# Mamba stage: the drive of every second pair of states made by VectorE in PSUM, with B spread by DMA, and A and the dt bias loaded plainly and placed by TensorE

## What is computed

```python
xz = h @ in_proj_w
u, z = jnp.split(xz, 2, axis=-1)
u = silu(causal_depthwise_conv(u, conv_w, conv_b))
xdbl = u @ x_proj_w                      # dt_r (64), B (16), C (16)
dt = softplus(dt_r @ dt_proj_w + dt_proj_b)
A = -jnp.exp(A_log)
def step(hst, inp):
    dt_t, B_t, C_t, u_t = inp
    dA = jnp.exp(dt_t[..., None] * A)
    dBu = dt_t[..., None] * B_t[:, None, :] * u_t[..., None]
    hst = dA * hst + dBu
    y = jnp.einsum('bdn,bn->bd', hst, C_t)
    return (hst, y)
y = (ys + u * D) * silu(z)
return y @ out_proj_w
```

## Time and profile before

| | |
|---|---|
| median of 3 runs | 2992.26 us (2989.83 to 2993.07) |
| the profiled execution | 2989.16 us, its span 2987.4 us |
| first scan starts | 814.89 us |
| scan of position 0 of the last item | 2618.08 us |
| mean clock granted to TensorE, of full speed | 0.961 |
| PE, DVE, ACT, POOL busy, share of the span | 89%, 79%, 62%, 61% |

### The profile page before, as it was taken

The page is one execution under the profiler, slowest core; times in us unless marked ns, Lnnn a source line. Parts: engine busy times, 40 slices in busy tenths (PEclk is TensorE's granted clock), DMA queues, the critical chain, the costliest instruction groups (busy, mean ns, idle before and its releaser), DMA issues. The chain is left out here.

```text
span 2987.4 us, 48154 instructions
## 1 busy us (share of the span) xinstructions
PE 2668.5 (89%) x17342; PEld 2127.1 (71%) x17342; DVE 2348.1 (79%) x2434; ACT 1848.3 (62%) x2524; POOL 1826.3 (61%) x1211
## 2 busy tenths in 40 slices
PE   5999996596699999999999999999999999985892
PEld 4878785464277878878778788777787887874561
DVE  6878874574389889899888898998988988894563
ACT  3565653254567777777677776776777767761451
POOL 1221211454477877878778787787787877784454
PEclk8999998798799999999999999999999999998896
DMA  1211212424402112022020120210202202103333
GB/s 49 64 49 56 63 36 56 112 75 116 159 1 78 47 39 86 9 79 73 14 86 23 64 86 1 85 64 23 86 8 79 86 1 78 45 27 89 90 103 102
DMA packets 137133, 186.07 MB, mean 62 GB/s; under 512 B 27800, under 2 KB 112664, under 8 KB 136920
## 3 DMA queue, kind: packets, MB, share of 16 engines
q1 hardware_dynamic: 129432, 162.69, 17.8%
q0 software_dynamic: 7488, 20.46, 2.7%
HBM read 141.13 MB, written 41.98 MB: 61 GB/s over the span
## 5 line engine op out<-in xcount | busy, mean ns | idle before, releaser
L1353 POOL TENSOR_TENSOR m_state<-m_state,m_c_all 128x1024 f32<-128x1024 f32 x512 | 1205.1, 2368 | 357.3 <-DVE m_state L1468 356.3
L1468 DVE TENSOR_TENSOR_SCAN m_state<-m_decay,m_ps_d 128x1024 f32<-128x1024 f32 x512 | 1162.1, 2278 | 145.0 <-issue 89.0
L1533 ACT ACTIVATE m_decay<-m_dt,m_aneg 128x511 f32<-128x511 f32 x1024 | 657.7, 710 | 30.1 <-DVE m_state L1468 26.6
L1768 PEld LDWEIGHTS m_ps_d<-m_bdiag,m_duT 128*128 128x128 f32 x4096 | 488.4, 192 | 105.9 <-issue 73.4
L1781 PE MATMUL m_ps_y<-m_ident,m_state 128*128 128x128 f32 x4096 | 533.1, 273 | 3.0 <-POOL m_state L1353 2.5
L1768 PE MATMUL m_ps_d<-m_bdiag,m_duT 128*128 128x128 f32 x4096 | 504.5, 276 | 29.4 <-DVE m_state L1468 23.6
L1781 PEld LDWEIGHTS m_ps_y<-m_ident,m_state 128*128 128x128 f32 x4096 | 463.6, 141 | 8.7 <-POOL m_state L1353 7.5
L1445 DVE TENSOR_TENSOR m_duB<-m_duT,m_ps_i 128x1024 f32<-128x1024 f32 x256 | 306.1, 1196 | 8.8 <-ACT m_duT L1561 8.8
L1766 PEld LDWEIGHTS m_ps_d<-m_ident,m_duB 128*128 128x128 f32 x2048 | 235.5, 141 | 76.9 <-issue 70.9
L1679 PE MATMUL m_ps_f<-m_hT,m_win 128*128 128x512 f32 x512 | 249.8, 612 | 36.0 <-ACT m_u L1574 17.9
L1766 PE MATMUL m_ps_d<-m_ident,m_duB 128*128 128x128 f32 x2048 | 265.8, 273 | 7.1 <-DVE m_state L1468 7.0
(11 more groups left out here) (201 smaller groups left out, 4407.0 us busy)
## 6 DMA issues: line engine op xcount, KB each, us to landing
m_c_all<-m_c_rows SPq DMA_DIRECT2D x128, 512.0 KB, 5.5
out<-m_xw SPq DMA_DIRECT2D x32, 512.0 KB, 2.9
f_y_rows<-f_y_sb SPq DMA_DIRECT2D x46, 256.0 KB
a_xin<-x SPq DMA_DIRECT2D x16, 512.0 KB, 4.8
a_xres<-x SPq DMA_DIRECT2D x16, 512.0 KB, 5.6
x<-a_xout SPq DMA_DIRECT2D x16, 512.0 KB, 3.3
m_xin<-x SPq DMA_DIRECT2D x16, 512.0 KB
m_xw<-out SPq DMA_DIRECT2D x16, 512.0 KB, 5.6
```

Of the source, the lines that this page charges most:

```text
L1353: nc.gpsimd.tensor_tensor(s, s, c_all[:, n, :, :], ALU.mult).then_inc(weighed, 1)
L1468: nc.vector.tensor_tensor_scan(state[:, r, :, :].rearrange("p n t -> p (n t)"), decay[:, r, :, :].rearrange("p n t -> p (n t)"), ps_d[i % ...
L1533: ins = nc.scalar.activation(decay[:, r, j, 1:S], dt_sb[:, c, 1:S], ACT.Exp, scale=aneg[:, c, n:n + 1])
L1768: ins = nc.tensor.matmul(drive_t, duT[:, c, t, :], bdiag[:, n // 2, TT * j + t, :], start=True, stop=True)
```

## The change

**Drives.** At even positions DVE now writes the drive itself: du, with channels on partitions, is copied by ScalarE into a PSUM bank (ps_u, `put_du`, once for each chunk), B of the pair stands in SBUF on all 128 partitions (b_all), and `scale` multiplies the two into ps_d[0]. TensorE makes only the odd positions, all into ps_d[1]. The 8 transposes at every even position are gone, and with them duB. dt and duT keep 2 chunks instead of 4.

**B.** It goes to DRAM beside C (8 small stores an item instead of 4) and comes back by 4 more DMAs of 512 KB an item (`b_pair`), each behind a `c_pair` in SP's queue.

**Diagonals.** DVE makes none. POOL makes two of the four tiles of an item at its positions 26 and 28, ScalarE the other two at its positions 0 and 3, each by 8 copies of 128x128 with B as scale.

**Start.** A_log and the bias are loaded as they lie, and TensorE places them by 20 small matmuls; 17 DMAs go, 2 come. Several parts of DVE, POOL and ScalarE stand one to three positions earlier or later.

```diff
@@ TURNS (also X, Y1, B, DT0 and O1 one later)
-        16: [("O", 0, -1)],
+        17: [("O", 0, -1)],
@@ start, SP
-            for r in range(Q):
-                for k in range(CT):
-                    sp.dma_start(aneg[CH * r:CH * r + CH, k, :].rearrange("c (q g) -> c q g", q=Q),
-                                 a_log[:, Q * k + r, :].rearrange("(c q) g -> c q g", q=Q)).then_inc(a_loaded, 16)
@@ SP
+            def b_pair(m):
+
+                sp.dma_start(b_all[:, m, :, :], bc_rows[0, 4 * m:4 * m + 2, :].partition_broadcast(P))\
+                    .then_inc(b_loaded[m], 16)
...
                     for n in range(NP - 2):
                         c_pair(st, 1, n)
+                        if n % 2 == 0:
+                            b_pair(n // 2)
@@ POOL
+                    if i in (26, 28) and st.has(1):
+                        diagonal(st, 1, i - 25)
@@ DVE
-                nc.vector.tensor_tensor(duB[:, r, :, :, :], duT[:, c, :, :].unsqueeze(1).to_broadcast([P, 2, TT, P]),
-                                        ps_bt[h][:, 2 * n:2 * n + 2, :].unsqueeze(3).to_broadcast([P, 2, TT, P]),
-                                        ALU.mult).then_inc(scaled, 1)
+                if n == 0:
+                    dve.wait_ge(du_put, CT * b + c + 1)
+                if c == 0:
+                    dve.wait_ge(b_loaded[n // 2], 16 * (b + 1))
+                if i >= 2 or st.has(o - 1):
+                    dve.wait_ge(scanned, UN * b + i - 1)
+                nc.vector.tensor_tensor(ps_d[0][:, :, :], ps_u[:, :].unsqueeze(1).to_broadcast([P, 2, S]),
+                                        b_all[:, n // 2, :, :], ALU.mult).then_inc(scaled, 1)
...
-                    if i % 2 and i + 3 < UN and st.has(0):
-                        scale(st, 0, i + 3)
-                    if i % 2 and i + 3 >= UN and st.has(1):
-                        scale(st, 1, i + 3 - UN)
+                    if i % 2 == 0 and i + 2 < UN and st.has(0):
+                        scale(st, 0, i + 2)
...
-                    if i in (23, 30) and st.has(1):
-                        dt_relu(st, 1, (23, 30).index(i))
-                    if i in (26, 28, 30) and st.has(1):
-                        diagonal(st, 1, i - 25)
+                    if i in (24, 30) and st.has(1):
+                        dt_relu(st, 1, (24, 30).index(i))
+                    if i == 30 and st.has(1):
+                        scale(st, 1, 0)
@@ ScalarE
+            def put_du(st, o, c):
+
+                b = st.item(o)
+                act.wait_ge(du_ready, CT * b + c + 1)
+                if c or st.has(o - 1):
+                    act.wait_ge(scaled, UN // 2 * b + NP // 2 * c)
+                nc.scalar.activation(ps_u[:, :], du_sb[:, c % 2, :], ACT.Copy).then_inc(du_put, 1)
...
+                for j in range(2):
+                    for t in range(TT):
+                        ins = nc.scalar.activation(bdiag[:, n // 2, TT * j + t, :], id_sb[:, :], ACT.Copy,
+                                                   scale=bt[h][:, 2 * n + j, t:t + 1])
...
+                    if i == 29 and st.has(1):
+                        put_du(st, 1, 0)
+                    if i in (0, 3) and st.has(0):
+                        diagonal(st, 0, 5 if i == 0 else 7)
@@ TensorE
-                    if i < UN - 1 and st.has(0):
+                    if i % 2 == 0 and st.has(0):
                         drive(st, 0, i + 1)
-                    if i == UN - 1 and st.has(1):
-                        drive(st, 1, 0)
```

More of the change, by code:

```diff
@@ L1464, in emit @@
                         dve.wait_ge(decay_ready, g + 1)
-                        dve.wait_ge(drive_full, g + 1)
+                        dve.wait_ge(drive_full if i % 2 else scaled, UN // 2 * st.item(0) + i // 2 + 1)
                         if i >= RING or st.has(-1):
@@ L1479, in emit @@
                         y_read(st, 0, (i - 9) // 8)
-                    if i == 0 and st.has(0):
-                        diagonal(st, 0, NP - 1)
                     if i in (9, 17) and st.has(0):
@@ L1485, in emit @@
                         gate(st, -1, 3)
-                    if i in (17, 23) and st.has(-1):
-                        b, v = st.item(-1), (i - 17) // 6
+                    if i in (18, 24) and st.has(-1):
+                        b, v = st.item(-1), (i - 18) // 6
                         dve.wait_ge(res_back, 16 * (b + 1))
@@ L1616, in emit @@
                         silu(st, z_sb, "Z", z_full, z_ready, (0, 1) if i == 25 else (2, 3))
-                    if i in (2, 12, 20) and st.has(0):
-                        to_duT(st, 0, 1 + (2, 12, 20).index(i))
-                    if i == 19 and st.has(1):
+                    if i in (2, 12, 21) and st.has(0):
+                        to_duT(st, 0, 1 + (2, 12, 21).index(i))
+                    if i == 20 and st.has(1):
                         b = st.item(1)
@@ L1626, in emit @@
                         nc.scalar.activation(xd[0:RX, :], f_bank("X", 0)[0:RX, :], ACT.Copy).then_inc(xd_ready, 1)
-                    if i == 21 and st.has(1):
+                    if i == 22 and st.has(1):
                         b = st.item(1)
@@ L1722, in turn @@
                     f = take(st, kind, k)
+                    if not st.has(0):
+                        pe.wait_ge(bias_set, 1)
                     pe.wait_ge(xd_ready, b + 1)
```

187 lines of the change are left out of this document (98 added, 89 removed).

## The result

Over 12 runs of each on one chip the changed kernel took 2979.03 us (2974.86 to 2986.48) against 2991.28 (2989.14 to 2993.48): a ratio of 0.9961, 95% interval 0.9953 to 0.9969. It is 12 us faster, where 72 were forecast, and lies 11 us above the range. On a second chip the same kernel came to 0.9977 (0.9967 to 0.9987). The profiled execution has a span of 2976.0 us and a mean clock of 0.941 (before: 0.961).

The account below looks back on a forecast made before the run. TensorE, 98% busy, was taken to bound the loop; 112.2 us plus 3.0 of stops gave 115.2 an item instead of 120.2, minus 75 over 15 items, plus 2.8 for first and last: 2917 profiled, 2920 median; range 2858 to 2968.

Parts of the forecast that it names:

- What bounds the kernel, and the prices: Loop: TensorE fills it, DVE next; scale 1.24 us, a POOL diagonal 2.4, an ACT piece 0.3.
- The sum over the intervals: Whole item: maxima of PE and DVE work over 16 two-position intervals, 112.2 us, plus 3.0 of stops, 115.2.
- new stops: DVE waits for the du copy behind softplus and for POOL's diagonals at y_read: 0 to 5 us an item, 3.0 taken.
- Cost nothing in the loop: Loads of B by DMA: they land in time for DVE, with 12 us sufficing; 1.5 us at the first item only.
- rival D: TensorE's granted clock falls in the loop; at a mean of 0.91 intervals grow by 5 us, gain gone; chance 0.03.
- A: Whole loop: all is hidden and DVE sets the pace, 109 us an item, 2830 us; chance 0.14.
- B: ScalarE becomes the bound if a 128x128 copy takes 0.5 us: up to 120.4 us an item, 2990 us; chance 0.14.
- C: B comes late at DVE's scale at position 30, every item; each microsecond beyond costs 15 us; chance 0.05.
- E: TensorE's transposes were already hidden, so no gain: 2992 us; chance 0.04.

Follow-up runs that it names:

- du_first: Changed kernel with ScalarE's copy of dt*u for the next item's first chunk moved ahead of the second softplus; 2962.38 us, 0.9972 of the kernel before.
- no_loop_du_first: Changed kernel with its 12-item loop written out without jumps and the dt*u copy moved ahead of the softplus; 2932.35 us, 0.9810 of the kernel before.
- no_loop: Changed kernel with the 12 items of its loop written out on all four engines, no jumps back; 2944.51 us, 0.9844 of the kernel before.
- diag_once: Changed kernel, loop written out and dt*u copy moved, with the diagonal tiles made for the first item alone; 2932.32 us, 0.9806 of the kernel before.

## Why the prediction was wrong

**What bounds the kernel, and the prices.** Right. PE is at 90% in the loop, scale, the diagonals and the copies cost what was said or less, and the last item grew by 2.2 us from its first to its last scan (forecast 1.3). The first scan came 1.3 us later (forecast 1.5, for the loads of B), but that is luck: DVE stood there 4.34 us for ACT's copy, and for B only 0.46 us at the scale behind it.

**The sum over the intervals, 115.2 us an item.** Nearly right as a law for an item without seam trouble: 115.2 to 116.2 in du_first ahead of its first jump, 115.9 in no_loop_du_first. The 3.0 us of new stops in it were right in kind (the copy behind softplus) but not in what they add up to: with the copy as it is, an item without a jump takes 117.3, so what was put at 3.0 comes to 5.1 by the same sum. That is 2.1 x 15 = 32 us of the missing 60. Part of it is the clock, for the drive behind the stop takes 2.9 to 3.8 us in place of 2.0 at 14 seams of no_loop. Moving the copy returns 12 net; of the other 20, 10 are the 0.7 us an item by which the count was too low (115.9), and 9 the two items in which the clock falls.

**"Cost nothing in the loop", said of the tiles of B, is the step that failed.** It asked when DVE wants the tile (12 us after the issue at the earliest; it landed in 6.4 to 11.0, no scale from 1000 to 1950 us waited for it) and left out who else uses the DMA engines just then. The code for the jump does. 5 jumps at 6 us more than before (7.2 against 1.2) are 30 us, the other half. The rows for it stood in the trace of before: TensorE's stops on "issue" at the loop's start, 1.15 and 1.39 us, and intervals that alternate between 119.7 and 121.1 to 121.8 us; the prediction took their mean, 120.2, and read no further.

**The clock.** The prediction held it at 1.00, with rival D at 3 in 100. It fell to 0.97 in the loop, by halving for some microseconds at nearly every seam and in some items once more, 80 us on. D as put (the gain cancelled by a mean of 0.91) is wrong, but its mechanism is real: 1.6 to 4.5 us for an item that it hits away from a longer stop.

**Rivals.** A (DVE-bound at 109) is excluded: DVE stands 10 us an item or more even with half of V left out. B (ScalarE bound): the price it rests on is 0.30, and diag_once shows the diagonals free; but its time came nearest to the result, by other causes. C: no tile was late but for the 0.46 us in the first item. E: had the transposes been hidden, nothing would have been gained, but without jumps the change as a whole is worth 38 us; what their going alone brings no run shows.

**The range** ended at 2968 because no rival was about a jump.
